# A graph network with expert layers on one core: chained scans and a bank a head in the edge softmax, routing with the weights stationary, expert biases by products, two norms moved into neighbouring programs

## The chip, the cores and the metric

The kernel runs on one NeuronCore of a Trainium2 chip. The metric is the device time of one execution in microseconds (us); lower is better. The engines are TensorE (PE; its weight loads are PEld), VectorE (DVE), ScalarE (ACT), GpSimd (POOL) and SyncE (SP), which only issues transfers. Each has its own instruction stream; they meet at semaphores.

## The reference

There are 1250 nodes of 768 features (`x`) and 40000 edges (`src`, `dst`), sorted by `dst`. Four residual layers follow one another, each on the layer norm of `x`:

```
x = x + gat(layernorm(x))      # GATv2, 8 heads, then GATv2 with 1 head, each with a softmax
                               # over the edges of one destination
x = x + soft_moe(layernorm(x)) # 32 experts x 32 slots: h = gelu(slots @ w1 + b1); eo = h @ w2 + b2
x = x + gcn(layernorm(x))      # two graph convolutions over the same edges
x = x + moe(layernorm(x))      # router 768 -> 8, softmax, top 2 of 8, expert: gelu(x @ w1 + b1) @ w2 + b2
```

The edge softmax is `ex = exp(logits - segment_max(logits, dst)[dst])`; its sum divides the messages later.

## The kernel before, in words

`program` (L2516) runs one sub-program after another. Each is a `Scope`: a block of five instruction streams, then a barrier of all engines and a clearing of its semaphores (L99), so nothing of the next one starts before the last engine of the present one is done. The order: `setup`, `norm_rows` ("ln0"), `project`, `logits`, `edge_softmax` of 8 heads, `aggregate`, `finish_project`, `logits`, `edge_softmax` of 1 head, `edge_sums`, `mix_soft`, `soft_slots`, `soft_experts`, `soft_combine`, `norm_counted`, `gcn_layers`, `norm_rows` ("ln3"), `route`, `experts`. Nodes lie in NB = 10 blocks of 128 rows, D = 768 in KD = 6 parts of 128.

`Chain` (L61) makes DVE wait for its own last instruction after each call.

- `setup` reads the edge lists, asks SP for `x` (L239, L240) and turns the lists into tiles of 128 edges and 332 visits (a tile met with a block of 64 nodes). DVE waits for TensorE's products at L318 and L331.
- `norm_rows` (L377): DVE takes 20 `bn_stats`, 10 `bn_aggr`, an inverse root with ACT's square root and one Newton step (L171), and 10 `tensor_scalar` that write `R.H` (L153).
- `edge_softmax` (L721): the logits of 332 visits are transposed so that 83 partitions hold 4 quarters (q) of visits with 128 edges each. PE's transposes go through a PSUM tile of two banks, ACT copies them into `S` (L803). DVE builds a penalty `pen` that is -1e30 between edges of different destinations, and takes a running maximum forward (L840) and backward (L841), both from `S`. The ends of the visits go through PE and DVE so that maxima carry from visit to visit (L875 to L898). In a second pass each quarter gets both scans again, the larger of the two (L902), the subtraction (L903), ACT's exponential (L810) and a product on POOL that zeroes edges of other blocks (L830). When all four quarters are masked, PE turns the result back: for each head four products over the quarters into one of two banks (L794), and ACT copies each head out (L814).
- `soft_experts` (L1689): 8 groups (g) of 4 experts. SP loads `w1` and `w2` of a group, two of each deep: the next `w1` after the group's hidden product (s_h), the next `w2` after its outer product (s_e). Biases are broadcast over 32 partitions by ACT's transfers, 4 of `b1` and 4 of `b2` a group (L1725, L1729). DVE adds `b1` to the hidden sums (L1768, L1769), ACT applies gelu, PE transposes (L1808), ACT copies, PE multiplies by `w2` (L1819), DVE adds `b2` (L1774). Between these PE transposes parts of `comb` (L1790).
- `gcn_layers` (L1890): mixes of rows by counts, then 20 products a layer, each of 12 instructions (L2107). DVE evicts each (`evict`: L1970 and, in the second layer, L1976). `R.low`, read by the mixes, lies where `R.H` lies.
- `route` (L2149): SP stores `R.H` and `R.X`. For each of 10 blocks ACT copies the rows (L2216), PE transposes six parts (L2332), DVE copies them out (L2230), and PE multiplies with the turned rows stationary and the 8 columns of the router moving (L2339), the bias by a product of one row (L2340); DVE copies the 8 logits (L2234). Then come the softmax over the 8 experts (from L2247), the top two and the lists.

Of the kernel before, what the change touches and what calls it, by code (L numbers as in the profile page):

```python
# [16 lines left out]
ALU = mybir.AluOpType  # L17
# [9 lines left out]
P = 128  # L27
# [165 lines left out]
def setup(nc, R, x, src, dst):  # L193


    LISTS = ((1, 6, NEAR_VISITS), (2, 7, PAIR_VISITS), (WIDE, 5, WIDE_VISITS))
    with Scope(nc, "set") as c:
# [24 lines left out]
        fetched = [ps[:, 2 * PAIR_VISITS:2 * PAIR_VISITS + WIDE_VISITS] for ps in (psP, psD)]  # L222
        s_zero, s_x, s_p = (c.sem(n) for n in ("zero", "x", "lists"))
# [22 lines left out]

        @block.gpsimd
# [13 lines left out]
        def _(dve):  # L261
            chain = Chain(dve, s_v)
            nc.vector.memset(rows[:, 0], 0).then_inc(s_zero, 1)
# [50 lines left out]
            chain(nc.vector.tensor_scalar(down[:], down[:], float(P), None, ALU.mult))  # L314

# [12 lines left out]
            nc.vector.memset(R.ends[:, :, :, P + 1:P + 2], NONE)  # L328

# [9 lines left out]
            chain(last)  # L339

# [31 lines left out]

def norm_rows(nc, R, name, l2=False):  # L377

    with Scope(nc, name) as c:
        W = Roots(c)  # L380
        sq = c.sb("squares", [P, NB, D]) if l2 else None
        s_v, s_row, s_sum = c.sem("v"), c.sem("row"), c.sem("sum")
        block = c.enter_context(nc.Block())

        @block.scalar
        def _(act):
            square_roots(nc, act, W, W.val, W.root)
            if l2:
                for b in range(NB):
                    act.wait_ge(s_row, b + 1)  # L390
                    nc.scalar.activation(sq[:, b, :], R.H[:, b, :], ACT.Square, accum_out=W.sq[:, b:b + 1]).then_inc(s_sum, 1)
                square_roots(nc, act, W, W.val, W.root)

        @block.vector
        def _(dve):
            chain = Chain(dve, s_v)
            layer_norms(nc, dve, chain, R.H, R.X, W, row=s_row, dealt=l2)
            if l2:
                dve.wait_ge(s_sum, NB)
                chain(nc.vector.tensor_copy(W.val[:], W.sq[:]))  # L400

                chain(nc.vector.tensor_scalar(W.val[:], W.val[:], 1e-24, None, ALU.max))
                inverse_roots(nc, dve, chain, W, W.val, W.root, W.rstd)
                for b in range(NB):
                    nc.vector.tensor_scalar(R.H[:, b, :], R.H[:, b, :], W.rstd[:, b:b + 1], None, ALU.mult)
# [315 lines left out]
def edge_softmax(nc, R, name, heads, summed):  # L721
# [10 lines left out]
    with Scope(nc, name) as c:  # L732
# [8 lines left out]
        psS = c.ps("psS", [P, 2, 4, P])  # L741
        psR = c.ps("psR", [heads, 4, BANK])
        psC = c.ps("psC", [P, BANK])
        s_v, s_turn, s_copied, s_side, s_rows, s_carry, s_back = (c.sem(x) for x in ("v", "turn", "copied", "side", "rows", "carry", "back"))
        s_exp, s_exped, s_ret, s_retd = c.sem("exp"), c.sem("exped"), c.sem("ret"), c.sem("retd")
        s_masked, s_empty, s_blank, s_numbers, s_turns = c.sem("masked"), c.sem("empty"), c.sem("blank"), c.sem("numbers"), c.sem("turns")
# [16 lines left out]
        def _(pe):  # L763
            for q in range(4):
                for h in range(heads):
                    n = q * heads + h
                    if n >= 8 and n % 4 == 0:
                        pe.wait_ge(s_copied, n // 4 - 1)
                    t = nc.tensor.transpose(psS[0:VQ, n // 4 % 2, n % 4, :], R.L[:, h, q * VQ:(q + 1) * VQ], R.ident[:])
                    if n % 4 == 3:  # L770
                        t.then_inc(s_turn, 1)
# [10 lines left out]
            for h in range(heads):  # L782
                if h == 0:
                    pe.wait_ge(s_masked, 4)
                if h >= 2:
                    pe.wait_ge(s_retd, h - 1)
# [1863 lines left out]
```

## Time and profile before

| | us |
|---|---|
| median of 3 runs (lowest, highest) | 4086.74 (4086.54, 4087.12) |
| the profiled execution: its own time / its span | 4087.04 / 4085.3 |
| busy: PE, DVE, ACT, POOL | 3594.3, 2356.2, 1502.1, 1346.9 |
| first norm, 48.2 to 67.8 | 19.6 |
| edge softmax of 8 heads, 769.3 to 877.2 | 107.9 |
| edge softmax of 1 head, 2001.9 to 2043.4 | 41.5 |
| slot experts, 2754.7 to 2870.3 | 115.6 |
| second norm, 3314.8 to 3333.7 | 18.9 |
| routing, 3333.7 to 3406 | 72.3 |

Durations come from the profiled execution, whose own time is 1.7 us more than its span; the runs are compared by their medians. An instruction's time in the timeline is from its start to its end; in a group (xN) from the first start to the last end. What stands in brackets is how long the engine had been idle and what ended that.

### The profile page before, as it was taken

What the parts mean: (1) busy time and instruction counts of PE and PEld (TensorE: products, weight loads), DVE (VectorE), ACT (ScalarE), POOL (GpSimd) and SP (SyncE); (2) the same over time, 40 slices, a digit from 0 to 9 for tenths busy, and PEclk for the clock granted to TensorE, in tenths of its full rate; (3) what the DMA queues carried; (4) which work ended last, traced back from release to release, by engine and by line L of the source; (5) the groups of instructions that cost most, each with busy time, mean ns of one, the idle gap of its engine ahead of it and who ended that gap; (6) DMA issues with size and microseconds to landing.
All of it is one profiled execution on the core that took longest, in us unless ns stands there. A gap on an engine that the chain in (4) does not pass through costs nothing. (4 is left out here: it accounts for less than half of the span.)

```text
span 4085.3 us, 73866 instructions
## 1 busy us (share of the span) xinstructions
PE 3594.3 (88%) x19021; PEld 2512.6 (62%) x19022; DVE 2356.2 (58%) x8267; ACT 1502.1 (37%) x4515; POOL 1346.9 (33%) x1388
## 2 busy tenths in 40 slices
PE   5979999559999897999666689996989977999998
PEld 3657777435555456777566655443557766887787
DVE  4459999968888767999889966502142132010110
ACT  0027777438888422222277723200021011111111
POOL 0136666247777116777366620000000000111110
PEclk9989999769999898999899999997999977999999
DMA  3258888438888428999487720009000027426261
GB/s 106 78 174 293 292 294 293 152 107 296 291 294 296 136 74 277 321 322 321 162 285 214 215 93 1 22 29 358 34 27 26 2 77 282 142 55 242 46 227 52
DMA packets 193146, 715.58 MB, mean 175 GB/s; under 512 B 31078, under 2 KB 54486, under 8 KB 192678
## 3 DMA queue, kind: packets, MB, share of 16 engines
q0 software_dynamic: 108608, 502.39, 38.1%
q1 hardware_dynamic: 81382, 208.22, 14.2%
q10 hardware_dynamic: 3072, 3.94, 0.4%
q8 instruction: 43, 0.70, 0.1%
q14 instruction: 41, 0.34, 0.0%
HBM read 781.56 MB, written 33.04 MB: 199 GB/s over the span
## 5 line engine op out<-in xcount | busy, mean ns | idle before, releaser
L708 PE MATMUL l_psZ<-X,ident 128*128 128x396 f32 (+3 forms) x2656 | 808.2, 426 | 0.0
L644 POOL DMA_INDIRECT X<-fs,near_src x664 | 630.5, 950 | 331.6 <-DVE l_psZ L665 299.2
L708 PEld LDWEIGHTS l_psZ<-X,ident 128*128 128x128 f32 x2656 | 498.1, 190 | 185.8 <-issue 2.2
L705 PE MATMUL l_psZ<-fd,l_spread 128*128 x1328 | 450.9, 421 | 49.0 <-ACT l_spread L621 49.0
L996 PE MATMUL a_psO<-a_g,a_sel 128*128 128x396 f32 (+1 forms) x1328 | 457.8, 503 | 11.7 <-DVE a_g L952 11.5
L979 ACT ACTIVATE a_g<-a_g,L 128x99 f32<-128x99 f32 x1328 | 374.0, 364 | 93.4 <-DMA a_g<-fs,pair_src 92.9
L934 POOL DMA_INDIRECT a_g<-fs,pair_src x332 | 355.2, 1070 | 125.7 <-issue 99.6
L996 PEld LDWEIGHTS a_psO<-a_g,a_sel 128*128 128x128 f32 x1328 | 237.4, 190 | 231.8 <-issue 72.1
L2499 PEld LDWEIGHTS r_psH<-r_rowsT,ew_w 128*128 128x128 f32 x2916 | 331.6, 193 | 8.4 <-issue 1.5
L2499 PE MATMUL r_psH<-r_rowsT,ew_w 128*128 128x128 f32 x2916 | 331.9, 276 | 1.1 <-DVE r_rowsT L2457 1.1
L671 DVE SCALAR_TENSOR_TENSOR l_zr<-l_psZ,l_attn 128x99 f32<-128x99 f32 x1660 | 323.9, 255 | 0.0
L2509 PE MATMUL r_psY<-ew_w,r_hT 128*128 128x384 f32 x972 | 318.0, 486 | 0.0
L678 DVE SCALAR_TENSOR_TENSOR l_zr<-l_psZ,l_attn 128x772 f32<-128x772 f32 x332 | 316.0, 952 | 0.0
L627 ACT ACTIVATE l_zr<-l_zr 128x99 f32<-128x99 f32 x996 | 270.1, 273 | 105.7 <-DVE l_zr L676 105.6
L1153 PE MATMUL a_psC<-a_sel,a_pick 128*128 128x96 f16 x2660 | 213.2, 207 | 101.4 <-DVE a_sel L1106 52.9
L705 PEld LDWEIGHTS l_psZ<-fd,l_spread 128*128 128x128 f32 x1328 | 238.2, 189 | 87.2 <-issue 67.4
L2509 PEld LDWEIGHTS r_psY<-ew_w,r_hT 128*128 128x128 f32 x972 | 182.6, 190 | 121.6
L665 DVE TENSOR_TENSOR l_psZ<-l_psZ,X 128x124 f32<-128x124 f32 (+1 forms) x664 | 219.6, 331 | 48.3 <-PE l_psZ L708 17.1
L1153 PEld LDWEIGHTS a_psC<-a_sel,a_pick 128*128 128x128 f16 x2660 | 174.7, 98 | 116.3 <-issue 100.5
L1051 POOL DMA_INDIRECT a_fetched<-eye,wide_src x206 | 207.7, 1008 | 104.1 <-PE a_psC L1153 74.1
L621 ACT ACTIVATE l_spread<-l_away,l_one 128x512 fp32r<-128x512 f32 x166 | 119.9, 722 | 323.8 <-PE l_psZ L708 320.9
L2442 ACT ACTIVATE r_hT<-r_psH,r_b1t 128x128 f32<-128x128 f32 x243 | 88.0, 367 | 380.9 <-PE r_psH L2499 380.7
(481 smaller groups left out, 5543.0 us busy)
## 6 DMA issues: line engine op xcount, KB each, us to landing
ew_w<-in_L_ffn_w SPq DMA_DIRECT2D x54, 3456.0 KB
l_dsts<-near_rows SPq DMA_DIRECT2D x166, 128.0 KB
room<-in_L_ffn_w SPq DMA_DIRECT2D x8, 2304.0 KB
hw_w<-in_L_ffn_w SPq DMA_DIRECT2D x24, 576.0 KB
X<-fs,near_src POOLq DMA_INDIRECT x664, 5.3
H<-in_L_ffn_b SPq DMA_DIRECT2D x27, 384.0 KB
X<-in_x SPq DMA_DIRECT2D x2, 3456.0 KB
a_g<-fs,pair_src POOLq DMA_INDIRECT x332, 4.6
```

What stands on the lines that cost most here:

```text
L627: last = nc.scalar.activation(cut, cut, ACT.Copy, accum_out=R.L[:, h, ds(n, 1)])
L644: nc.gpsimd.indirect_dma_start(out=g[:, n % RING, :], out_offset=None, in_=fs, in_offset=bass.IndirectOffsetOnAxis(ap=R.near_src[:, n:n + ...
L671: nc.vector.scalar_tensor_tensor(out=zr[:, k, lo:hi], in0=psZ[k][:, lo // half, lo % half:lo % half + he], scalar=0.0, in1=at[:, lo:hi], o ...
L678: last = nc.vector.scalar_tensor_tensor(out=zr[:, k, :].rearrange("p (a e) -> p a e", a=2), in0=psZ[k][:, :, 0:half], scalar=0.0, in1=at[: ...
L705: nc.tensor.matmul(psZ[k][:, a, 0:half], spread[:, j // 4, k, :], R.fd[:, ds(b, 1), lo:hi].squeeze(1), start=True, stop=True)
L708: last = nc.tensor.matmul(psZ[k][:, a, 0:hi - lo], R.ident[:], g[:, j, lo:hi], start=False, stop=True, skip_group_check=True)
L934: nc.gpsimd.indirect_dma_start(out=g[:, n % RING, 0:width], out_offset=None, in_=table, in_offset=bass.IndirectOffsetOnAxis(ap=R.pair_src[ ...
L979: last = nc.scalar.activation(rows, rows, ACT.Copy, scale=R.L[:, h, ds(v * 2 + 1, 1)])
L996: last = nc.tensor.matmul(psO[j][:, a, 0:hi - lo], sel[:, j, k, :].bitcast(F32), g[:, j * 2 + k, lo:hi], start=(k == 0), stop=(k == 1))
L1153: last = nc.tensor.matmul(to, own, sel[:, j, k].rearrange("p k q -> p (k q)"), start=(k == 0), stop=(k == WIDE - 1))
L2499: last = nc.tensor.matmul(psH[m % 4][:, 0:P], w1t[s][:, k, m * P:(m + 1) * P], rowsT[s][:, k, :], start=(k == 0), stop=(k == KD - 1))
L2509: last = nc.tensor.matmul(psY[:, a, 0:HALF], hT[s][:, m, :], w2t[s][:, m, a * HALF:(a + 1) * HALF], start=(m == 0), stop=(m == KH - 1))
```

## The change

**Norms.** `norm_rows` goes. Its first use is taken into `setup`: the statistics of three blocks before L318's wait, the other seven, the means and the inverse roots before L331's wait, the ten `tensor_scalar` at the end. Its second use goes into `gcn_layers`: each eviction of the second layer is followed by its `bn_stats`, and the blocks are normalised in three groups.

**Edge softmax.** The backward scan reads the forward scan's result, so that its own result is the segment's maximum, and L902 goes; one instruction takes `max(run, -1.25e29) - S`, and the exponential has scale -1. Edges of other blocks get 1e30 less in the copy out of PSUM, which DVE now makes (8 instructions of 512 columns), and POOL's product goes. `pen` is no longer cleared as a whole; its backward half is written by ACT. The transposes use a bank for each four; on the way back each head has its own bank, and PE goes quarter by quarter.

**Slot experts.** Both biases are loaded once; a 0/1 matrix `belongs` (32 partitions) multiplies them into PSUM ahead of the products. ACT's gelu reads PSUM, DVE only copies the outer sums.

**Routing.** PE transposes straight from `R.H`; the router's 8 columns are stationary and up to 512 turned rows move; DVE adds the bias on 8 partitions; ten small transposes bring the logits back.

```
 def setup:
+            dve.wait_ge(s_x, 32)
+            statistics(0, EARLY)                      # EARLY = 3
             dve.wait_ge(s_lists, 1)
...
+            statistics(EARLY, NB)
+            for b in range(NB):
+                last = nc.vector.bn_aggr(W.mv[:, b, :], W.st[:, b])
+            chain(last)
+            chain(nc.vector.tensor_scalar(W.val[:], W.mv[:, :, 1:2].squeeze(2), 1e-5, None, ALU.add))
+            inverse_roots(nc, dve, chain, W, W.val, W.root, W.rstd)
             dve.wait_ge(s_lists, 2)
...
+            for b in range(NB):
+                nc.vector.tensor_scalar(R.H[:, b, :], R.X[:, b, :], W.mv[:, b, 0:1], W.rstd[:, b:b + 1], ALU.subtract, ALU.mult).then_inc(s_normed, 1)
 def edge_softmax, PE:
-            for h in range(heads):
-                if h == 0: pe.wait_ge(s_masked, 4)
-                if h >= 2: pe.wait_ge(s_retd, h - 1)
-                for q in range(4):
-                    last = nc.tensor.matmul(back[:, lo:hi], S[:, q, h, 1:P + 1], turn[:, q, lo:hi], start=(q == 0), stop=(q == 3), skip_group_check=True)
+            for q in range(4):
+                pe.wait_ge(s_exped, q + 1)
+                for h in range(heads):
+                    t = nc.tensor.matmul(banks[:, h, lo:hi], S[:, q, h, 1:P + 1], turn[:, q, lo:hi], start=(q == 0), stop=(q == 3), skip_group_check=True)
 ACT:
+            for q in range(4):
+                nc.scalar.copy(pen[:, 1, q, :, 1:P], bcast(same[:, q], 1, heads)).then_inc(s_pen, 1)
+                nc.scalar.activation(S[:, q, :, 1:P + 1], S[:, q, :, 1:P + 1], ACT.Exp, scale=-1.0).then_inc(s_exped, 1)
 POOL:
-                nc.gpsimd.tensor_tensor(w, w, bcast(R.valid[:, q, :], 1, heads), ALU.mult).then_inc(s_masked, 1)
 DVE:
-            chain(nc.vector.memset(pen[:], 0.0))
+            nc.vector.tensor_scalar(lost[:], R.valid[:], -1.0, -NEG, ALU.add, ALU.mult)
+            chain(nc.vector.tensor_tensor(same[:], e[:, :, 2:P + 1], e[:, :, 1:P], ALU.not_equal))
+            chain(nc.vector.tensor_scalar(same[:], same[:], NEG, None, ALU.mult))
+            for n in range(heads):
+                last = nc.vector.tensor_tensor(to, banks[0:VQ, n, :].rearrange("p (a b) -> p a b", a=4), less, ALU.add)
-                    scan(run[:, 1] reversed, pen[:, 1, q], S[:, q])
+                    scan(run[:, 1] reversed, pen[:, 1, q], run[:, 0])
-                chain(nc.vector.tensor_tensor(run[:, 0], run[:, 0], run[:, 1], ALU.max))
-                chain(nc.vector.tensor_tensor(S[:, q, :, 1:P + 1], S[:, q, :, 1:P + 1], run[:, 0, :, 1:P + 1], ALU.subtract))
+                chain(nc.vector.scalar_tensor_tensor(out=w, in0=run[:, 1, :, 1:P + 1], scalar=NEG / 8, in1=w, op0=ALU.max, op1=ALU.subtract))
 def soft_experts:
+            for half in range(2):
+                act.dma_start(b1t[half * EXPERTS:(half + 1) * EXPERTS, :], b1).then_inc(s_b1, 16)
+                act.dma_start(b2t[half * EXPERTS:(half + 1) * EXPERTS, :], b2).then_inc(s_b2, 16)
-                nc.scalar.activation(h[:], h[:], ACT.Gelu).then_inc(s_gelu, 1)
+                nc.scalar.activation(h[:, 0:HID], psH[g % 2][:, 0:HID], ACT.Gelu)
+                nc.scalar.activation(h[:, HID:2 * P], psH[g % 2][:, 0:SHARED], ACT.Gelu).then_inc(s_gelu, 1)
+                nc.tensor.matmul(psH[g % 2][:, 0:HID], mine, b1t[rows, :], start=True, stop=False, skip_group_check=True)
+                for a in range(2):
+                    nc.tensor.matmul(psE[g % 2][:, a, 0:HALF], mine, b2t[rows, a * HALF:(a + 1) * HALF], start=True, stop=False, skip_group_check=True)
 def gcn_layers:
+                    last = nc.vector.bn_stats(R.st[:, b, a, :], R.X[:, b, cut])     # in evict, second layer
+            for g in range(len(GROUPS)):                                            # (0, 7), (7, 9), (9, 10)
+                for b in range(*GROUPS[g]):
+                    for a in range(2):
+                        evict(1, b, a)
+                inverse_deviations(g)        # bn_aggr, root by ACT, Newton step, of the group
+                normalise(g)                 # waits for the last mix, then tensor_scalar a block
 def route:
+            for b in range(6):
+                turn(b)
+            multiply(0)                      # 6 products, 8 columns stationary, 512 rows moving
+            for b in range(6, NB):
+                turn(b)
+            multiply(1)
+            multiply(2)                      # the last 256 rows
+            back(0, 4)
+            back(4, 8)
+            back(8, NB).then_inc(s_back, 1)
 program:
-            norm_rows(nc, R, "ln0")
-        norm_rows(nc, R, "ln3")
```

## Rows read from the trace of the kernel before

**Rows 1.** The page, part 1: busy time, share of the span, instructions by engine.

```profile
PE 3594.3 (88%) x19021; PEld 2512.6 (62%) x19022; DVE 2356.2 (58%) x8267; ACT 1502.1 (37%) x4515; POOL 1346.9 (33%) x1388
```

**Rows 2.** Windows (start:end, length, busy time by engine, TensorE clock, DMA share, GB/s).

```profile
25.00:30.00 5.00, 5.00 (x19) 4.13 (x18) 3.22 (x13) 0.00 (x0) 0.00 (x0) 1.00 0.10 28
...
856.50:876.50 20.00, 19.42 (x64) 15.70 (x64) 0.00 (x0) 3.49 (x8) 0.00 (x0) 0.50 0.00 0
...
2790.00:2840.00 50.00, 32.85 (x317) 15.56 (x321) 10.00 (x18) 3.14 (x15) 0.00 (x0) 0.78 1.03 367
...
3182.00:3189.00 7.00, 7.00 (x41) 4.21 (x39) 0.00 (x0) 1.40 (x3) 0.00 (x0) 1.00 0.00 0
...
3334.00:3380.00 46.00, 43.85 (x200) 43.12 (x200) 11.41 (x22) 9.50 (x11) 0.57 (x4) 0.50 0.45 171
```

**Rows 3.** Timeline of the set-up, the first norm and the start of the projection.

```profile
13.73 0.41 SPq L239 DMA_DIRECT2D X<-in_x  x1
...
32.46 1.12 DVE L318 TENSOR_SCALAR set_local<-set_near_dst,set_shift 83x128 bf16<-83x128 f32 x4 [3.93 <-PE set_near_src L357]
...
45.69 0.50 DVE L331 CAST pair_src<-set_pair_src 128x332 int32<-128x332 f32 x1 [9.08 <-PE set_turned L370]
...
49.14 9.30 DVE L132 BATCH_NORM_STATS2 ln_st<-X 128x6 f32<-128x384 f32 x20 [1.00 <-PEq L99]
...
60.95 5.98 DVE L153 TENSOR_SCALAR H<-X,ln_mv,ln_rstd 128x768 f32<-128x768 f32 x10
...
67.78 2.73 SPq L438 DMA_DIRECT2D p_w<-in_L_gnn_W1s  x6
```

**Rows 4.** Timeline of the edge softmax of eight heads.

```profile
771.14 6.99 DVE L845 MEMSET s_pen<- 83x8320 f32 x1 [3.78 <-issue]
...
785.03 0.68 DVE L852 COPY s_pen<-s_run 83x1016 f32<-83x1016 f32 x1
...
787.33 2.32 DVE L840 TENSOR_TENSOR_SCAN s_run<-s_pen,s_S 83x1040 f32<-83x1040 f32 x1
...
826.95 3.20 POOL L830 TENSOR_TENSOR s_S<-s_S,valid 83x1024 f32<-83x1024 f32 x1 [55.13 <-ACT s_S L810]
...
828.21 4.11 DVE L841 TENSOR_TENSOR_SCAN s_run<-s_pen,s_S 83x1040 f32<-83x1040 f32 x1
...
851.89 1.22 DVE L903 TENSOR_TENSOR s_S<-s_S,s_run 83x1024 f32<-83x1024 f32 x1
...
856.55 19.42 PE L794 MATMUL s_psS<-turn,s_S 83*128 83x332 f32 x64 [38.42 <-POOL s_S L830]
...
876.00 0.44 ACT L814 COPY L<-s_psS 128x332 f32<-128x332 f32 x1 [1.95 <-PE s_psS L794]
```

**Rows 5.** Timeline of the edge softmax of one head: one scan, and its last products.

```profile
2009.48 0.42 DVE L840 TENSOR_TENSOR_SCAN s_run<-s_pen,s_S 83x130 f32<-83x130 f32 x1
...
2037.69 4.58 PE L794 MATMUL s_psS<-s_turn,s_S 83*128 83x316 f32 x8 [8.31 <-POOL s_S L830]
```

**Rows 6.** Slot experts: DMA queues of 2750 to 2880, and a wait.

```profile
q10 hardware_dynamic: 3072, 3.94, 11.2%
...
PE m_psE L1819 <- DMA room<-in_L_ffn_w: 24.6, 6, 4.5
```

**Rows 7.** Timeline of the last eviction of the convolution, last part of the norm.

```profile
3312.62 0.62 DVE L1970 SCALAR_TENSOR_TENSOR room<-gc_psO,dinv,gc_bias 128x384 f32<-128x384 f32 x1 [2.66 <-PE gc_psO L2107]
...
3326.64 5.98 DVE L153 TENSOR_SCALAR H<-X,ln_mv,ln_rstd 128x768 f32<-128x768 f32 x10
```

**Rows 8.** Timeline of the routing, and of the 512-column products of slots.

```profile
2744.74 8.75 PE L1679 MATMUL m_ps<-disp,normed 128*128 128x512 f32 x20
...
3341.62 1.54 PE L2332 MATMUL r_psT<-ident,r_rows 128*128 128x128 f32 x6
...
3343.20 0.96 DVE L2230 COPY r_rowsT<-r_psT 128x768 f32<-128x768 f32 x1 [1.19 <-PE r_psT L2332]
...
3379.93 0.24 DVE L2247 TENSOR_REDUCE r_red<-r_probs 128x10 f32<-128x80 f32 x1
```

More of the change, by code:

```diff
@@ L245, in _ @@
             sp.wait_ge(s_p, 64)
+        @block.scalar
+        def _(act):
+            square_roots(nc, act, W, W.val, W.root)
         @block.gpsimd
@@ L371, in _ @@
             last.then_inc(s_lists, 1)
[L377 to L405, printed above, removed]
 def project(nc, R, name, weights, table, biases, attn, heads):
@@ L858, in _ @@
                 nc.vector.tensor_copy(sides[:, q, 2, :], R.ends[:, 0, q, 1:2].broadcast_to([VQ, heads]))
-                chain(nc.vector.tensor_copy(sides[:, q, 3, :], R.ends[:, 0, q, P:P + 1].broadcast_to([VQ, heads])))
+                nc.vector.tensor_copy(sides[:, q, 3, :], R.ends[:, 0, q, P:P + 1].broadcast_to([VQ, heads]))
             if summed:
@@ L1950, in _ @@
                 for m, (lo, hi) in enumerate(CHUNKS):
+                    if n and m == 2:
+                        square_root(0)
                     if n or m:
@@ L2152, in route @@
     with Scope(nc, name) as c:
-        w, bias, one = c.sb("w", [P, KD, ME]), c.sb("bias", [1, ME]), c.sb("one", [1, P])
-        rows = [c.sb(f"rows{s}", [P, D]) for s in range(2)]
-        rowsT = [c.sb(f"rowsT{s}", [P, KD, P]) for s in range(2)]
+        w, bias = c.sb("w", [P, KD, ME]), c.sb("bias", [ME, 1])
+        restT, lg = c.sb("restT", [P, KD, ROWS - 2 * BANK]), c.sb("lg", [ME, ROWS])
+        cols = [weights.first[1][:, :, 0:BANK], weights.first[1][:, :, BANK:2 * BANK], restT[:]]
         pr, best = c.sb("probs", [P, NB, ME]), c.sb("best", [P, NB, ME])
@@ L2210, in _ @@
         def _(act):
-            act.sem_inc(s_turn, 2)
-            with act.Fori(0, NB // 2) as i:
-                for s in range(2):
-                    b = i * 2 + s
-                    act.wait_ge(s_turn, b + 1)
-                    nc.scalar.copy(rows[s][:], blk(R.H, b)).then_inc(s_rows, 1)
             act.wait_ge(s_sub, 1)
@@ new lines, in back @@
+            def back(lo, hi):
+                pe.wait_ge(s_logit, lo // 4 + 1)
+                for b in range(lo, hi):
+                    last = nc.tensor.transpose(psB[:, b, :], lg[:, b * P:(b + 1) * P], R.ident[0:ME, 0:ME])
+                return last
+            for b in range(6):
[7 more added lines that the diff above has]
+            back(4, 8)
```

257 lines of the change are left out of this document (133 added, 124 removed).

## The prediction

> **What bounds the kernel now.** I read the page's busy shares first: TensorE is busy for 88% of the span and every other engine for 58% or less [rows 1]. That is an average over sub-programs that barriers keep apart, so I then read the timeline of each edited one. The reader is to see three kinds. In the first norm [rows 3] and the second [rows 7] VectorE alone works and all else waits. In the edge softmax [rows 4] the path is a chain of DVE instructions, and after it a chain of TensorE products that begins only when everything is masked. In the slot experts the DMA share is full (1.03) while PE is busy for 33 of 50 us [rows 2]: transfers set the pace. In the routing PE is busy for 43.9 of 46 us, at a granted clock of 0.50, which is 1.2 GHz [rows 2]. None of the edits touches the logits, the aggregation or the last experts, where most of the time goes; those shift as they are.
>
> **First norm.** DVE is idle 3.93 us before L318 and 9.08 us before L331 [rows 3]. These two gaps are the room for what moves: 20 statistics take 9.30 us, 0.465 each; six of them are 2.8 us, in the first gap, if `x` is there. Its transfer is asked for at 13.73 [rows 3] and DMA is down to 28 GB/s after 25 us [rows 2], so it is. Fourteen are 6.5 us, and means and roots 60.95 - 49.14 - 9.30 = 2.5: together 9.0, against 9.08 of idle time. ACT's square root is only in this chain and has nothing before it on its queue. The ten last instructions (5.98) stay on the path, at the end of the set-up. So the time from 48.14 (the barrier before the norm begins) to 60.95 goes: 12.8, less 0.2 because 9.0 and 9.08 are nearly equal. Low end: nothing fits in the second gap's last 2.5 us, 10. I take **12.6**. The weights asked for at 67.78 come earlier by as much; nobody waits for anything else.
>
> **Edge softmax of 8 heads** [rows 4]. Preparation now runs from 771.14 to 787.33, 16.2 us. Gone: the memset (6.99), four backward copies (0.68 each, now ACT's, during DVE's other work), and the copies out by ACT turn into DVE work. New on DVE, at L903's rate of 1.22 us for 1024 columns: three instructions of 512 (1.8), four forward copies (2.7), small memsets and ends (some 1.3 by what is left of the old 16.2), eight sums of 512 out of PSUM (4.9): 10.7. Saved 5.5. The transposes before them no longer wait and take some 7 us beside 5.8 us of DVE's preparation, so part of the eight may wait for PE: low end 4.5.
>
> The first pass costs the same: a scan that reads another scan's result is as long. In the second pass a quarter has 2.32 + 4.11 + two operations of 1.22 to 1.24. One of the two goes in all four quarters: 5.0. The 4.11 stands in three quarters, and there the scan starts (828.21) while POOL's product (826.95 to 830.15) runs; elsewhere the same scan takes 2.32. Without POOL I expect 2.32: 3 x 1.8 = 5.4. Between the last subtraction (ends 853.11) and the first product (856.55) are 3.4 us of exponential and mask; an exponential of 1024 columns is some 1.3 (three times the 0.44 of 332 columns), so 2.1 goes. Then 64 products take 19.42 and one copy 0.44. New: only the last quarter's 16 products follow the last exponential; at the mean of 0.30 they are 4.9, and they are the narrow ones (103 columns; the mean is of 170), so 3.3 to 4.9, and a copy: 4.4. The other 48 fit beside the scans: the widest quarter's 16 take some 9 us, of two quarters of 6 us. Saved 15.5. Sum: 5.5 + 5.0 + 5.4 + 2.1 + 15.5 = **33.5** (28 to 36).
>
> The Trainium skill ("SBUF — State Buffer", section "SBUF: two separate sides") says that GpSimd and a VectorE instruction with two SBUF inputs exclude each other. By that rule the 5.4 is a wait for POOL and goes whole; if the 4.11 had another cause it would be 0 and the sum 28.
>
> **Edge softmax of 1 head.** The last products, 4.58 us for eight [rows 5], keep two of eight on the path: 3.4. The second pass loses the mask and one small operation a quarter, some 0.3 each by the scan of 130 columns (0.42): 2. The preparation loses chained waits and a 0.9 us memset: 1.8. **7.2** (3.4 to 9).
>
> **Slot experts.** The broadcasts are queue q10: 3.94 MB and 11.2% of the engines' time in 130 us, 14.6 us [rows 6]; four loads of 0.25 MB in all take their place. By bytes at the stretch's 367 GB/s [rows 2] it is 10. I take **12** (3 to 14). The cover: PE gets six more instructions a group, but it waits 24.6 us in six waits for `w2` alone [rows 6], so a chain longer by some 1 us a group is hidden, and it costs up to 8 us if it were not. What is late first: the first hidden product now waits for `b1` from HBM, queued beside two `w2` loads; the old chain waited for the same bias one step later, so nothing is lost. SP's next loads hang on those products, two deep, and the queue stays full.
>
> **Second norm** [rows 7]. An eviction has 2.66 us idle before it, so two statistics' 0.47 to 0.6 fit without delaying PE, which waits only for L1970. The seven-block group is normalised right after the last mix (4.2 us, while PE makes block 7's first half), the next two before the last eviction. On the path after the last eviction (3312.62 + 0.62 + 0.6 = 3313.8): statistic 0.5, means and root 1.8, one block 0.6: 3316.7. Before, the norm ended at 3326.64 + 5.98 = 3332.6. **15.9** (14.5 to 16.5).
>
> **Routing** [rows 8]. From 3332.6 to L2247 at 3379.9 is 47.3 us. New, at 1.2 GHz: barrier 1.1; six blocks' transposes at 1.54, 9.2 (DVE's 0.96 a block hides). A product of 512 columns is two instructions; 20 instructions take 8.75 at the high clock, so a group of 12 takes 5.3 at 2.4 GHz and 10.5 at 1.2. The rest: four blocks 4.8, a group of 512, one of 256 (2.6 or 5.3), small ends 0.9. If the clock never rises: 1.1 + 9.2 + 10.5 + 6.3 + 10.5 + 5.3 + 0.9 = 43.8, saving 3.5. If it rises inside the first group and is partly lost over the transposes: 1.1 + 9.2 + 7.9 + 4.8 + 6.5 + 2.6 + 0.9 = 33.0, saving **14.3**.
>
> Does it rise? PE's 8-column products left it at 0.50 for 46 us. Products on 83 partitions filled 19.4 of 20 us and it stayed at 0.50. Products on all 128 partitions with 32 stationary columns kept it at 1.00 [rows 2]. The new ones are on 128 partitions, without gaps, with 8 stationary columns. I read the rows as: partitions count, stationary columns do not; 6 to 4 for a rise.
>
> The Trainium skill ("TensorE: Matmul & The Clock Gate", sections "What's actually happening" and "Part 4: PE-mode transpose") says that sustained work releases the clock, and that transposes do not count as such work. The first half speaks for the rise, but the softmax's products disagree with it as it stands; the second speaks against this change, because four blocks of transposes lie between two groups. By the first alone the routing would save some 17, with the second some 14.
>
> **Sum.** 12.6 + 33.5 + 7.2 + 12 + 15.9 + 14.3 = 95.5. From the profiled execution's own 4087.0: 3991.5; the median lies 0.3 lower: **3991 us**.
>
> **Rivals.**
> 1. The clock stays at 1.2 GHz in the routing: the columns that are stationary count after all. The sum is 84.7, the time 4002. For it: no row shows so few columns at a raised clock. Chance 0.33.
> 2. The experts' chain takes over from the transfers: hidden product, gelu, transposes, copies, outer product and now six more instructions. For it: at the low clock the outer products double. Against it: the waits of [rows 6]. The saving is 3 instead of 12: 4000, with rival 1 4011. Chance 0.1.
> 3. The scans' 4.11 is not POOL's doing, or the chained scan is slower; the softmax saves 28 or less: 3997. Chance 0.04.
> 4. Slower: DVE's longer evictions become the bound of the convolution. An eviction comes each 3.87 us (0.62 + 0.6 + 2.66 and gaps) and would take some 1.9. It decides from 3.87 on, and it would have to take 3.87 + 95/20 = 8.6 us to eat the gain: 4087 or more. Nothing near it is in the rows. 0.01. That the change does not do what it says (a wait left that keeps a norm or the mask in place): 0.01.
> The forecast has 0.51.
>
> **Range.** 3977 to 4011: below, the upper ends of the softmax, the experts and a clock kept in the routing (2.5 + 2 + 2 and the small ones, some 14 in all if they meet); above, rivals 1 and 2 together. Within 0.2% (8 us, about what a measurement of this kernel can tell) of no change only by rival 4's neighbours: faster 0.98, same 0.01, slower 0.01.
>
> **What the new profile should show.** No stretch of statistics between the set-up and the projection, and L331's successor starting by 46.3. Second-pass scans of 2.32 in all four quarters, PE's last 16 products ending 5 us after the last exponential. No queue q10 of 3.9 MB, the experts' stretch near 103 us with the DMA share still full. Three us from the last eviction to the end of `gcn_layers`. In the routing 12-instruction groups of 5 to 8 us and a granted clock over 0.5; groups of 10.5 mean rival 1. I am wrong if DMA is idle in the experts, if evictions come later than each 3.87 us, or if the set-up's lists wait for statistics.

## The result, and the profile of the changed kernel

The changed kernel takes 3974.81 us (median of four runs, 3973.8 to 3976.4), the kernel before 4086.77 on the same chip: a ratio of 0.9724, with a 95% interval of 0.9713 to 0.9735. It is 112 us faster. The forecast was 3991, with a range of 3977 to 4011: the direction was right, and 16 us of the gain were not seen; the time lies 2 us below the low end.

The profiled execution took 3975.72 us of its own, 111.3 less than that of before. The page, part 1 (busy time and share of the span by engine), answers to [rows 1]:

```profile
PE 3579.6 (90%) x18975; PEld 2485.5 (63%) x18976; DVE 2339.2 (59%) x8246; ACT 1492.4 (38%) x4487; POOL 1331.8 (34%) x1380
```

TensorE is busy 14.7 us less, and the span is 111.4 shorter: most of the gain is time in which TensorE stood idle. (The routing is the exception: there TensorE itself was the path.) Where it went is read by taking, in both traces, the start of the instruction that opens each stage. The differences between these starts are the whole account:

| stage, from its first instruction to the next stage's | saved, us | forecast |
| --- | --- | --- |
| set-up and first norm (to `p_w` at 67.78, now 55.17) | 12.6 | 12.6 |
| projection and logits | -0.8 | 0 |
| edge softmax, 8 heads (to the aggregation's first gather) | 34.3 | 33.5 |
| edge softmax, 1 head, and what lies between | 7.9 | 7.2 |
| slot experts (to the combine's first product) | 19.6 | 12 |
| combine and convolution | -0.2 | 0 |
| second norm (last eviction to the last normalised block) | 15.8 | 15.9 |
| routing (to the first reduction of the logits) | 21.4 | 14.3 |
| lists and last experts | 0.8 | 0 |

The sum is the 111.4 us between the two spans, and two lines hold the miss: the experts 7.6, the routing 7.1. I show the lines that were right briefly and the other two at length.

**First norm.** The timeline of the changed kernel's set-up (start, time, engine, line, operation, idle time before it and its releaser) answers to [rows 3]:

```profile
45.71 0.50 DVE L354 CAST pair_src<-set_pair_src 128x332 int32<-128x332 f32 x1 [0.23 <-PE set_turned L396]
...
55.17 0.83 SPq L430 DMA_DIRECT2D p_w<-in_L_gnn_W1s  x2
```

The 9.08 us of idle time before the pair lists have become 0.23, and the lists start within 0.02 us of where they did. The projection's first load follows the ten normalisations as it followed the old norm, 12.61 earlier.

**Edge softmax of 8 heads.** Its timeline answers to [rows 4]:

```profile
769.55 2.32 DVE L819 TENSOR_TENSOR_SCAN s_run<-s_pen,s_S 83x1040 f32<-83x1040 f32 x1
...
815.23 2.32 DVE L820 TENSOR_TENSOR_SCAN s_run<-s_pen,s_run 83x1040 f32<-83x1040 f32 x1
...
823.66 1.22 DVE L891 SCALAR_TENSOR_TENSOR s_S<-s_run,s_S 83x1024 f32<-83x1024 f32 x1
824.97 1.06 ACT L794 ACTIVATE s_S<-s_S 83x1024 f32<-83x1024 f32 x1 [5.02 <-DVEq L892]
...
826.08 3.74 PE L780 MATMUL s_banks<-turn,s_S 83*128 83x103 f32 x16 [2.18 <-ACT s_S L794]
```

Each term can be read off. From the sub-program's first instruction to the first scan it was 769.34 to 787.33 and is 757.50 to 769.55: 5.9 saved (forecast 5.5). From the first scan to the last subtraction it was 65.8 us and is 55.3: 10.5 (10.4). From there to the first product that nothing can hide, 3.4 and 1.2: 2.2 (2.1). And only 16 of 64 products stand behind the last exponential, 3.74 us in place of 19.42, so that the copies end at 830.29: 15.7 (15.5). That is 34.3.

**Slot experts.** The windows of the changed kernel (start:end, length, busy time of PE, weight load, DVE, ACT, POOL, TensorE's clock, DMA share, GB/s) answer to the third of [rows 2]; below them the DMA queues between 2705 and 2789 (packets, MB, share), and what PE waited for from 2695 to 2800 (us in total, times, longest), which answer to [rows 6]:

```profile
2700.00:2710.00 10.00, 1.10 (x6) 0.67 (x10) 1.00 (x3) 0.09 (x1) 0.00 (x0) 0.57 0.84 253
2710.00:2720.00 10.00, 9.14 (x79) 4.84 (x79) 1.38 (x2) 2.36 (x7) 0.00 (x0) 0.67 1.03 405
2720.00:2725.00 5.00, 5.00 (x74) 2.47 (x66) 0.96 (x1) 0.00 (x0) 0.00 (x0) 0.81 0.61 199
...
2750.00:2789.00 39.00, 32.45 (x359) 18.11 (x357) 9.70 (x13) 4.27 (x24) 0.00 (x0) 0.96 1.01 399
2789.00:2797.00 8.00, 5.20 (x44) 2.31 (x42) 2.28 (x4) 0.04 (x1) 0.00 (x0) 1.00 0.03 11
```

```profile
q1 hardware_dynamic: 9413, 32.08, 98.1%
q10 hardware_dynamic: 144, 0.22, 1.0%
```

```profile
PE m_psH L1774 <- DMA m_b1t<-in_L_ffn_b: 9.4, 1, 9.4
PE m_psH L1778 <- DMA w<-in_L_ffn_w: 4.5, 2, 2.3
...
PE m_psE L1802 <- DMA room<-in_L_ffn_w: 0.6, 2, 0.3
```

The DMA share is as full as before, but a full share now moves 399 to 405 GB/s and moved 367. The waits for `w2` fell from 24.6 us to 0.6. Not all of the 19.6 us is transfers. Here are the last group's outer products, which follow the last weights, before and in the changed kernel:

```profile
2862.47 4.94 PE L1819 MATMUL m_psE<-room 128*32 128x384 f32 x32 [4.30 <-DMA room<-in_L_ffn_w]
```

```profile
2791.06 2.79 PE L1802 MATMUL m_psE<-room 128*32 128x384 f32 x32 [0.29 <-DMA room<-in_L_ffn_w]
```

From the first issue (2754.74, now 2700.72) to these products it was 107.7 us and is 90.3: 17.4 saved. The other 2.2 lie behind the last weights, where the same 32 instructions take 2.79 us for 4.94. New in the stage is one wait of 9.4 us for the hidden biases at the very start, and the share drops to 0.61 between 2720 and 2725, because SP asks for the next weights when a group's products are done and the first group is late.

**Second norm and routing.** The timeline answers to [rows 7, 8]. The last eviction begins at 3239.22 and the last block is normalised by 3243.43:

```profile
3239.22 0.62 DVE L1965 SCALAR_TENSOR_TENSOR room<-gc_psO,dinv,gc_bias 128x384 f32<-128x384 f32 x1 [1.09 <-PE gc_psO L2128]
...
3242.75 0.68 DVE L1994 TENSOR_SCALAR H<-X,gc_mv,gc_total 128x768 f32<-128x768 f32 x1
...
3244.45 3.68 PE L2345 MATMUL r_psT<-ident,H 128*128 128x128 f32 x18 [5.27 <-PEq L99]
...
3251.03 5.32 PE L2356 MATMUL r_psL<-ew_w,r_w 128*8 128x512 f32 x12
...
3260.52 5.32 PE L2356 MATMUL r_psL<-ew_w,r_w 128*8 128x512 f32 x12
...
3269.31 0.24 DVE L2262 TENSOR_REDUCE r_red<-r_small 128x10 f32<-128x80 f32 x1 [0.38 <-PE r_small L2362]
```

Windows of the same stretch, with the columns as above:

```profile
3243.20:3244.00 0.80, 0.00 (x0) 0.00 (x0) 0.23 (x1) 0.00 (x0) 0.00 (x0) 1.00 0.00 0
...
3244.40:3247.20 2.80, 2.75 (x13) 2.61 (x14) 0.96 (x1) 1.28 (x1) 0.80 (x5) 0.50 0.49 145
3247.20:3247.60 0.40, 0.40 (x4) 0.40 (x3) 0.32 (x1) 0.00 (x0) 0.00 (x0) 0.55 1.05 415
...
3251.00:3269.00 18.00, 16.97 (x70) 6.22 (x69) 6.51 (x9) 0.00 (x0) 0.00 (x0) 1.00 0.86 332
```

The reader is to see the clock, the number behind the five busy times. It falls to 0.50 at 3244.2, 5 us after the last product (which ended at 3239.2), and is back at 1.00 by 3247.6, when TensorE has done nothing but transposes for 3.1 us. Both groups of 12 instructions take 5.32 us, which is their time at 2.4 GHz.

### The profile page after: what moved, and what is told of

It is laid out like the page before. It is cut to its first block and busy times, and to the rows that moved or that the text cites. A ratio compares the mean times of both kernels' runs of the same rounds, so it can differ in the third digit from the quotient of the medians.

```text
span 3973.9 us, 73505 instructions
## 1 busy us (share of the span) xinstructions
PE 3579.6 (90%) x18975; PEld 2485.5 (63%) x18976; DVE 2339.2 (59%) x8246; ACT 1492.4 (38%) x4487; POOL 1331.8 (34%) x1380
## 3 DMA queue, kind: packets, MB, share of 16 engines
q1 hardware_dynamic: 81396, 208.22, 14.4%
```

## The experiments

Times are medians; each comparison is with the kernel before on the same chip.

### Is the routing's gain the shorter wait in front of it, or what TensorE does in it?

In the changed kernel TensorE is idle for 5 us before the routing, before it was 23. Two kernels separate the edits. The first is the kernel before with the second norm folded in and the old routing:

```
 def gcn_layers:   as in the changed kernel
 def route:        as before
-        norm_rows(nc, R, "ln3")
```

> The kernel before with the second norm folded into the convolution and nothing else changed; the routing is the old one. Two theories of why the routing saved 21.4 us in the changed kernel and not the 14.3 forecast. Theory A, the idle time in front: TensorE now waits 5 us and not 20 before the routing, so the clock is hardly lost. Then the old routing, too, would run at 2.4 GHz here and end some 20 us earlier on top of the norm's 15.9: about 4050 us. Theory B, what TensorE does inside the routing: the old mix of transposes and products of 8 moving columns keeps the clock at 0.50 whatever stands in front. Then only the norm's 15.9 go: about 4071 us, and the routing still takes 47 us.

Measured: 4072.79 us, ratio 0.9961 (0.9947 to 0.9975), 15.4 us saved. The second is the kernel before with the new routing alone:

```
 def gcn_layers:   as before
 def route:        as in the changed kernel
         norm_rows(nc, R, "ln3")
```

> The kernel before with the new routing and nothing else changed, so TensorE stands idle for 20 us in front of it at a granted clock of 0.50. Theory A, the idle time in front decides: the clock stays low over the six blocks of transposes (9.2 us at 1.2 GHz) and rises only inside the first group of products or never; the routing saves 3.5 to 14.3: 4072 to 4083 us. Theory B, the new instruction mix decides: the clock rises during the transposes some 3 to 4 us after TensorE starts, as in the changed kernel, and the saving is about 21: 4066 us.

Measured: 4066.16 us, ratio 0.9949 (0.9932 to 0.9966), 22.0 us saved. Windows of the two routings, first the old one behind 7.8 us of idle time, then the new one behind 21:

```profile
3346.00:3356.00 10.00, 10.00 (x48) 9.90 (x48) 2.91 (x5) 2.74 (x3) 0.00 (x0) 0.50 0.00 0
```

```profile
3334.60:3338.60 4.00, 3.71 (x18) 3.56 (x18) 1.83 (x2) 1.28 (x1) 0.81 (x5) 0.50 0.56 175
...
3339.00:3339.40 0.40, 0.40 (x5) 0.40 (x5) 0.36 (x1) 0.00 (x0) 0.00 (x0) 1.00 1.05 415
...
3342.00:3359.00 17.00, 15.97 (x60) 5.55 (x58) 5.82 (x7) 0.00 (x0) 0.00 (x0) 1.00 0.90 343
```

Theory B holds in both. The old routing stays at 0.50 from end to end (47.5 us, before 47.3), though it is reached sooner. The new one comes to 1.00 after 4.1 us of transposes, from 21 us of idleness, and takes 26.3 us, in the changed kernel 25.9. The wait in front is worth less than a microsecond.

### The swap of operands, or the order?

The changed kernel with its new order, but with the old kind of product:

```
-                    last = nc.tensor.matmul(psL[g % 2][:, 0:hi - lo], w[:, k, :], cols[g][:, k, 0:hi - lo], ...)
+                for b in range(lo // P, hi // P):
+                    for k in range(KD):
+                        nc.tensor.matmul(psB[:, b, :], cols[g][:, k, b % 4 * P:(b % 4 + 1) * P], w[:, k, :], ...)
+                    last = nc.tensor.matmul(psB[:, b, :], one[:], bias[:], start=False, stop=True)
```

> The changed kernel with the order of the new routing (six blocks of transposes, four blocks' products, four blocks of transposes, the rest) but with the old kind of product: the transposed rows stationary, the 8 columns of the routing weights moving, the bias as a seventh product. It tells the swap of operands from the reordering and the two row copies that went. Theory A, the products with 8 moving columns pull the clock down to 1.2 GHz: the routing takes 42 to 46 us instead of 25.9, 3993 us. Theory B, the order alone let the clock rise and the swap is worth little: 140 products at some 0.15 us are 20 us instead of 13.4, the routing takes 31 to 33 us, 3981 us.

Measured: 3985.66 us, ratio 0.9753 (0.9736 to 0.9769), 11 us slower than the changed kernel. The routing takes 38.3 us (3241.5 to 3279.8). Its windows, and the products of one block early and late (12 instructions each):

```profile
3250.00:3255.00 5.00, 5.00 (x35) 4.89 (x34) 0.26 (x1) 0.00 (x0) 0.00 (x0) 0.80 1.02 395
3255.00:3260.00 5.00, 5.00 (x24) 4.93 (x25) 0.00 (x0) 0.00 (x0) 0.00 (x0) 0.50 1.03 404
3260.00:3265.00 5.00, 5.00 (x32) 4.67 (x31) 3.83 (x4) 0.00 (x0) 0.00 (x0) 0.68 0.86 313
```

```profile
3249.10 1.40 PE L2344 MATMUL r_small<-r_w,ew_w 128*128 128x8 f32 x12
...
3255.26 2.73 PE L2344 MATMUL r_small<-r_w,ew_w 128*128 128x8 f32 x12
...
3263.45 1.40 PE L2344 MATMUL r_small<-r_w,ew_w 128*128 128x8 f32 x12
```

The clock is at 1.00 when the products begin and at 0.50 before the fourth block; the transposes bring it back (3263.45 runs at 1.40 us again), and the products lose it once more. So neither theory is wholly right: the new order and the dropped row copies are worth 9.0 us of the 21.4 (no run tells these two apart), and the swap 12.4. How much of that is the clock can be estimated from the rows: the first block starts at 3249.10 and the second at 3250.75, so ten blocks at 1.00 would be 16.5 us, and the new products with their small transposes take 14.3 (5.32, 5.32, 2.75 and 0.92). Some 2 us would be left for the swap at the same clock; the other 10 are that it keeps the clock.

### Can the 5 us in front of the routing be covered?

This kernel has the early bias of the run further below, and 24 transposes of the identity after the convolution's last product:

```
+            for _ in range(24):
+                nc.tensor.transpose(psY[0][:, 0:P], R.ident[:], R.ident[:])
```

> The changed kernel with the hidden biases loaded early (3.2 us less in its own run) and with 24 transposes of the identity into a free PSUM bank after the convolution's last product, while VectorE finishes the last block of the second norm. TensorE then waits some 2 us instead of 5 before the routing. If the idle time is what brings the clock down at 3244, the first 18 transposes run at 2.4 GHz instead of 1.2 and the routing ends 1.8 us earlier: 3970 us with the early bias. If the clock falls there anyway, 3972 us.

Measured: 3972.13 us, ratio 0.9718 (0.9705 to 0.9732), the same as with the early bias alone (3971.62). The windows around the routing's start:

```profile
3238.20:3240.20 2.00, 0.06 (x1) 0.00 (x0) 1.47 (x6) 0.01 (x1) 0.00 (x0) 1.00 0.00 0
...
3240.60:3243.80 3.20, 2.89 (x14) 2.75 (x15) 1.01 (x2) 1.28 (x1) 0.80 (x5) 0.50 0.47 144
```

The last product ended at 3235.6, the transposes at 3238.3, and the clock fell at 3240.4, 2.2 us after the transposes and 4.8 after the products; in the changed kernel, without them, it falls 5.0 after the products. They bought nothing. But the run does not tell whether the transposes counted for the clock, because the delay of the fall is not the same in all traces. In the other fourteen, none of which has them, the clock falls 4.8 to 5.0 us after the convolution's last product in eleven and 2.1 us after it in three. One of the three is the run with the old products in the new order, where the last product ended at 3237.3:

```profile
3237.30:3239.30 2.00, 0.00 (x0) 0.00 (x0) 1.87 (x4) 0.00 (x0) 0.00 (x0) 1.00 0.00 0
3239.30:3239.50 0.20, 0.00 (x0) 0.00 (x0) 0.17 (x2) 0.00 (x0) 0.00 (x0) 0.58 0.00 0
```

A fall 4.8 us after the products fits the eleven, and the same fall 2.2 us after the transposes fits the three. Whether transposes can hold the clock stays open.

### What did the broadcasts cost in the slot experts?

The new slot experts alone, in the kernel before:

> The kernel before with the new slot experts and nothing else changed. If the 19.6 us that this stage saved in the changed kernel are its own, the time is 4067 us and the stretch from the first weights' issue to the combine is 96 us; if part of it came from what the other edits shifted, the time lies nearer to the forecast 12: 4075 us.

Measured: 4069.21 us, ratio 0.9955 (0.9938 to 0.9972), 19.0 saved: the gain is the stage's own. From SP's first issue to the combine's first product it takes 94.9 us, in the changed kernel 96.2, before 115.8. Then three kernels with the old chain and other transfers. First, each bias is loaded once:

```
-                if g + 1 < G:
-                    hidden_bias(g + 1)
...
-                if g + 1 < G:
-                    act.wait_ge(s_out, g + 1)
-                    outer_bias(g + 1)
...
-                dve.wait_ge(s_b1, 64 * (g + 1))
+                dve.wait_ge(s_b1, 64)
...
-                dve.wait_ge(s_b2, 64 * (g + 1))
+                dve.wait_ge(s_b2, 64)
```

> The kernel before; its slot experts load the broadcast biases for the first group of four experts alone and use them for all eight groups, so that seven eighths of the 3.9 MB are never moved (the output has the wrong biases). The chain of TensorE, ScalarE and VectorE instructions is the old one. Theory A, transfers: the broadcasts cost their own 14.6 us of DMA time and slow the weights' packets beside them from 140 to 154 ns, some 8 us more; seven eighths of both less what the chain takes over is 17 to 19: about 4069 us. Theory B, the broadcasts cost only their own share of time or bytes (10 to 14.6) and the rest of the 19.6 came from the new chain (bias products that keep TensorE's clock up, fewer additions on VectorE): 9 to 12.8 saved, 4074 to 4078 us, with the weights' packets still at 154 ns or the outer products still the bound.

Measured: 4067.08 us, ratio 0.9948 (0.9931 to 0.9965), 21.1 saved, with no other edit. By the interval that is at least 14, so theory B (9 to 12.8) is out and theory A (17 to 19) lies inside. The old chain, too, gets faster without the broadcasts: its outer products take 534 ns in the mean, where it was 766. Second, the outer biases alone are loaded once, the hidden ones as before:

> The kernel before; its slot experts load the outer biases (rows of 3 KB on 128 partitions) for the first group alone and use them for all eight, while the hidden biases (rows of 768 bytes) are still broadcast for every group. The output has the wrong outer biases. Both together once instead of eight times saved 21 us. If the cost goes by bytes, the outer ones are 3.15 of 3.94 MB, 80%: 17 saved, 4071 us. If it goes by packets (768 bytes in one, 3 KB in two), they are two thirds: 14 saved, 4074 us. If the small rows are what hurts, half or less: 10 saved, 4078 us.

Measured: 4070.64 us, ratio 0.9962 (0.9947 to 0.9976), 15.7 saved. The stage takes 99.3 us, with both once 95.2: 16.5 of 20.6 us, 80%, which is the outer biases' share of the bytes. One trace each does not part this from a cost by packets (two thirds, 13.7), since the stage of one and the same design varies by up to 3 us between traces; that the small rows alone are the cost (half or less) is not borne out. The third reads other rows of the same sizes:

```
-                    act.dma_start(b1t[32 * j:32 * j + 32, :], b1[g * 4 + j].partition_broadcast(32)).then_inc(s_b1, 16)
+                    act.dma_start(b1t[32 * j:32 * j + 32, :], hidden_weights.w1[g * 4 + j][0:32, :]).then_inc(s_b1, 16)
...
-                    act.dma_start(b2t[32 * j:32 * j + 32, :], b2[g * 4 + j].partition_broadcast(32)).then_inc(s_b2, 16)
+                    act.dma_start(b2t[32 * j:32 * j + 32, :], w2[g * 4 + j][0:32, :]).then_inc(s_b2, 16)
```

> The kernel before; in the slot experts each of the 64 bias transfers reads 32 different rows of the weights instead of one row 32 times, with the same sizes, targets and waits (the biases added are wrong ones). Theory A, bytes and packet sizes cost the time: no difference, 4088 us, and the weights' packets beside them still take 154 ns. Theory B, reading one row again and again is what is slow: most of the 21 us that the transfers cost goes, down to the 10 that bytes alone would be, 4077 us, and the packets of this queue take less time each.

Measured: 4086.95 us, ratio 1.0002 (0.9993 to 1.0012): no difference. Reading one row 32 times is not what costs. (Its stage is 113.5 us and before it was 115.8, but up to the last group's outer products both take about 107.7.) The queues of four kernels, each over 2765 to 2835 (packets, MB, share of 16 engines), in the order before, plain rows, outer biases once, both once:

```profile
q1 hardware_dynamic: 6538, 22.54, 89.7%
q10 hardware_dynamic: 2121, 2.56, 13.5%
```

```profile
q1 hardware_dynamic: 6520, 22.67, 89.9%
q10 hardware_dynamic: 2112, 2.56, 13.2%
```

```profile
q1 hardware_dynamic: 7783, 26.68, 99.1%
q10 hardware_dynamic: 1197, 0.66, 3.4%
```

```profile
q1 hardware_dynamic: 8070, 27.82, 101.5%
q10 hardware_dynamic: 68, 0.12, 0.7%
```

Divide the share by the packets: 0.897 x 16 x 70 us / 6538 is 154 ns for a packet of the weights before, 154 with plain rows, 143 with the hidden biases alone, 141 with neither. Beside the biases each weights' packet takes 13 ns longer; for the 9,400 packets of the stage on 16 engines that is 7.6 us, on top of the 14.6 us of the biases' own packets. Together 22 us are taken off the DMA engines, and up to the last group's outer products 18.4 of them are saved in the run with both biases once and 17.4 in the changed kernel. The 2.1 to 2.2 us behind that, in both runs, are the last products at the higher clock. Why a packet takes longer beside the biases is open.

### Does the first hidden product's wait cost anything?

The changed kernel with the two loads of the hidden biases issued in the sub-program before (`b1t` allocated one scope further out):

```
 def soft_slots:
+            for half in range(2):
+                act.dma_start(b1t[half * EXPERTS:(half + 1) * EXPERTS, :], b1).then_inc(s_b1, 16)
 def soft_experts:
-                act.dma_start(b1t[half * EXPERTS:(half + 1) * EXPERTS, :], b1).then_inc(s_b1, 16)
```

> The changed kernel, but the two loads of the hidden biases are issued at the start of the sub-program before the slot experts and land there, so that the first hidden product does not wait 9.4 us for them. If TensorE's late start is what held the later weight loads back (the DMA share drops to 0.61 between 2720 and 2725), the stage ends 3 to 6 us earlier: 3970 us. If the transfers pace the stage whatever TensorE does at its start, less than 1 us goes: 3975 us.

Measured: 3971.62 us, ratio 0.972 (0.9704 to 0.9737). Since the interval is wider than the gain, it was run again beside the changed kernel:

> The changed kernel itself, once more, on the same chip as the next run, so that the two can be compared with each other and not only through the kernel before: 3975 us.

> The changed kernel with the hidden biases loaded before the slot experts, once more, beside the changed kernel itself. Its trace showed a stage of 92.9 us instead of 96.2. If that is the whole effect the time is 3.2 us below the changed kernel's; if the stage only varies by that much from run to run, the two agree within 1 us.

Measured: 4144.33 and 4140.48 us, beside 4254.04 for the kernel before (all three took 4% longer than in the other comparisons, for a reason that no run shows, so only the ratios are read: 0.9741, 0.9728 to 0.9755, and 0.9733, 0.972 to 0.9747). The waits of PE in the first of these early runs:

```profile
PE m_psH L1780 <- DMA w<-in_L_ffn_w: 7.0, 3, 2.3
...
PE m_psH L1776 <- DVE room L1744: 2.3, 1, 2.3
```

The 9.4 us are 2.3, but PE's waits for weights rise from 5.8 us (4.5 for `w`, 0.7 and 0.6 for the others) to 9.2: half of what was won comes back. The stage takes 92.9, 92.9 and 94.4 us in the three traces that have the early bias, and 93.4 to 96.5 us (mean 95.3) in the six traces that have the new stage without it. So some 2 us are to be had, both times the median was 3 to 4 us lower, and the intervals of the whole kernel overlap: likely, not shown. The transfers set the pace here, and TensorE's late start costs only the dip in them.

### Were the softmax's terms right for the right reasons?

Its sum was hit, but a sum can be hit by errors that cancel. The changed kernel, with its products held back until all exponentials are done:

```
+            pe.wait_ge(s_exped, 4)
             for q in range(4):
```

> The changed kernel, but in both edge softmaxes TensorE waits for the exponentials of all four quarters before the first product, as the kernel before did. The prediction gave 14.5 of the softmax's 34.3 us to the products that run beside the scans. If so, 48 of 64 products of 0.30 us come back on the path: 14.4 us, and in the softmax of 1 head three quarters of 1.1 us, 3.4: together 3991 to 3993 us. The rival: the products are shorter together or the copies hide them, under 8 us: below 3983 us.

Measured: 3997.13 us, ratio 0.978 (0.9765 to 0.9795), 22.3 slower; its profiled execution, at 3995.41, is 19.7 slower. From the end of the last subtraction to the aggregation's first gather it takes 22.5 us and not 6.8, 15.7 more; in the softmax of 1 head, up to the next sub-program's first instruction, it takes 6.2 and not 3.1. The products are again one block:

```profile
825.29 19.42 PE L781 MATMUL s_banks<-turn,s_S 83*128 83x332 f32 x64 [25.74 <-ACT s_S L795]
```

The expected 14.4 and 3.4 are confirmed within 1.3 us, and the 15.7 are the whole of the term that the prediction put at 15.5. (The medians differ by some 3 us more than the two stretches; the intervals are wide enough for that.) Then GpSimd's product was put back, into a tile that nobody reads:

```
+            for q in range(4):
+                pool.wait_ge(s_exped, q + 1)
+                if q:
+                    pool.wait_ge(s_idle, q)
+                nc.gpsimd.tensor_tensor(idle[:], S[:, q, :, 1:P + 1], bcast(R.valid[:, q, :], 1, heads), ALU.mult).then_inc(s_idle, 1)
```

> The changed kernel with one addition: GpSimd multiplies each finished quarter by the mask into a tile that nobody reads, beside the next quarter's scans, as it did in place in the kernel before. Nobody waits for it but GpSimd. If the 4.11 us that a scan took there were GpSimd's doing, three scans of the softmax of 8 heads go from 2.32 to 4.11 us again and the time is 3980 us (the softmax of 1 head adds some 0.3). If the 4.11 had another cause that went with the change, the scans stay at 2.32 and the time at 3975 us.

Measured: 3979.08 us, ratio 0.9741 (0.9726 to 0.9756), 4.3 slower, where some 5 were expected (four runs, 3977.5 to 3987.5). The interval overlaps that of the changed kernel, so the time alone shows nothing; the rows that decide are the scans':

```profile
806.61 2.32 DVE L827 TENSOR_TENSOR_SCAN s_run<-s_pen,s_S 83x1040 f32<-83x1040 f32 x1
...
807.69 3.21 POOL L817 TENSOR_TENSOR s_idle<-s_S,valid 83x1024 f32<-83x1024 f32 x1 [47.86 <-ACT s_S L796]
...
808.96 4.12 DVE L828 TENSOR_TENSOR_SCAN s_run<-s_pen,s_run 83x1040 f32<-83x1040 f32 x1
```

The same three rows stand in each of the three later quarters, and from the sub-program's first instruction to the aggregation's first gather it takes 79.6 us and not 74.2, 5.4 more, which is three scans of 4.12 for 2.32. They show more than a slow scan. GpSimd's product begins inside the first scan, which keeps its 2.32 and ends at 808.93; the product ends at 810.90, 1.97 later (alone, as in the last quarter, it takes 2.18); and the second scan ends at 813.08, 2.18 after that. Each waits for the other: the longer times are waiting and not slower work. This is the exclusion that the Trainium skill states ("SBUF — State Buffer", section "SBUF: two separate sides"), and the trace agrees.

## Why the prediction was right, and where it was wrong

**What bounds each stage** was read rightly, and so were four of six terms, to 0.8 us: the room for the statistics before the lists, the second norm's path behind the last eviction, and the softmax term by term. Rival 3 (the 4.11 is not GpSimd's) is excluded by the run above; so is rival 4, since combine and convolution together lost 0.2 us.

**The experts' term was mis-sized.** The step said that the broadcasts take "11.2% of the engines' time in 130 us, 14.6 us", that by bytes it would be 10, and took 12. Both are prices of the broadcasts alone. What they did to the packets beside them was put at nothing, without a reason. The rows gave only one side of it: 367 GB/s at a share of 1.03 [rows 2], with no full share free of biases to compare. The runs show 14.6 us of the biases' own and some 7.6 through the others' packets, of which 17.4 came off the time, and 2.2 us more behind the last weights, where TensorE's clock was higher; neither of these two was in the sum. The 19.6 lie outside the term's own range (3 to 14) too, and so the low end of the whole range, which allowed the experts 2 us, was too high. The sign of "what is late first" was right: the hidden biases are late, and "nothing is lost" holds but for some 2 us at most, which the early load may have won back. Rival 2, in which the chain takes over, needed PE's waits for weights to be gone for long stretches. They nearly are (24.6 to 0.6 for `w2`), but from 2725 on the share stays full until 2789. TensorE's clock is 0.96 to 1.00 there, where it was 0.78, and its outer products take 519 ns and took 766, so the chain got faster just when it was needed. That it did so because it was no longer stopped is my reading; the run with both biases once, which has the old chain and 534 ns, speaks for it.

**The routing's term failed at one step**: "If it rises inside the first group and is partly lost over the transposes". The clock rose during the first six blocks' transposes, before any product, and was not lost over the four blocks later. By terms the six blocks took 6.6 us for 9.2, the first group 5.3 for 7.9, the four blocks 4.2 for 4.8, the group of 512 5.2 for 6.5; the rest agreed. With nothing but transposes, 3.1 us of them in the changed kernel and 4.1 in the run with the routing alone, the clock went from 0.50 to 1.00. The forecast had taken the lower of two values by the rule of the Trainium skill ("TensorE: Matmul & The Clock Gate", section "Part 4: PE-mode transpose") that transposes do not count as work; these two rows speak against it, and the run with 24 transposes in front of the routing does not decide it.

That the clock rose at all, against rival 1, was partly luck: the prediction argued from the new products, and the clock was up before the first of them ran. It did name the row that matters: the old mix, in which 14 of a block's 20 instructions move 8 columns, stayed at 0.50 with PE busy for 43.85 of 46 us [rows 2]. It did not forecast that the transposes without these products would raise the clock by themselves. The run with the old products in the new order then showed the clock fall from 1.00 to 0.50 within three blocks of them. A busy engine does not have the clock for that alone.

## What to carry to other kernels

A full DMA share is not a full rate: divide it by the packets of each queue, and price a small transfer by what it does to its neighbours too; here the broadcasts were 11% of the bytes, and without them the stage took 18% less. When the routing weights, or any narrow operand, multiply many rows, make the narrow one stationary: here TensorE was 95% busy at 1.2 GHz with 8 moving columns, and with 512 it ran at 2.4 GHz. Products that need only a quarter of the data belong behind that quarter, and an operation of GpSimd that nobody waits for can still cost VectorE 1.8 us a quarter, as it did here.

## What the hardware showed that was not expected

- Transposes alone raised the granted clock from 0.50 to 1.00, after 3.1 us in the changed kernel and 4.1 after 21 us of idleness. Behind the convolution's last product the clock fell after 4.8 to 5.0 us in eleven traces and after 2.1 in three; whether transposes in that gap put off the fall is open.
- With products of 8 moving columns TensorE was busy all the time, and the clock fell from 1.00 to 0.50 some 4 us after they began (3249.1 to 3253.0 in the run with the old products in the new order).
- Weights' packets of 3.4 KB in the mean took 141 ns alone and 154 beside 768-byte and 3 KB rows on another queue, whether these read one row 32 times or 32 rows. Why they slow down is open.
- VectorE's scan and GpSimd's product take strict turns: the scan of 1040 columns takes 2.32 us alone and 4.12 with the rest of a product in front of it, and the product, begun inside a scan, does its work only when the scan has ended, though neither touches a tile that the other writes.
